# Two output projections as three products of rounded halves, with the waits around them cut finer

## The chip, the cores and the metric

One core of a Trainium2 chip. The time is that of the device for one call of the kernel, in microseconds (us), median of three runs; less is better.

## What is computed

The input x is 8 images of 512 channels and 32 x 32 pixels. Two layers follow each other, both of the form x + attention(group norm(x)):

```python
# layer 0: dense attention over the 1024 pixels, 8 heads of 64
qkv = xs @ Wqkv + bqkv
scores = einsum('bhqd,bhkd->bhqk', q, k) / sqrt(64)
out = einsum('bhqk,bhkd->bhqd', softmax(scores), v)
out = out @ Wout + bout                        # first output projection
# layer 1: deformable attention in 4 x 4 windows of 8 x 8 pixels
xn = layer norm over channels; q = grouped 1x1 of xn (8 groups of 64)
off = tanh(pw(gelu(depthwise 6x6 stride 4 of q))) * 4   # 4 sample points per window and group
kv = grid_sample(xn, off); k, v = grouped 1x1 of kv
bias = MLP(128, 128, 1) of sign(pos) * log1p(|pos|)
out = einsum('bhij,bhdj->bhdi', softmax(q k + bias), v)
out = einsum('bchw,oc->bohw', out, w_out) + b_out       # second output projection
```

All arrays are float32.

## The kernel before

P = 128 partitions; the 512 channels are CT = 4 tiles. The kernel is written by hand engine by engine: each engine's block (`block.sync` for the DMA queue SP, `block.gpsimd` POOL, `block.tensor` PE, `block.scalar` ACT, `block.vector` DVE) is a Python function that issues that engine's instructions in the order in which it runs them, and semaphores tie them together. So an order is changed by moving a call, and a wait by `wait_ge`.

The main loop on every engine runs over the 8 images i. Image i's first attention runs together with rests of image i - 1's second one:

- **First attention**, 32 steps n (4 pairs of heads, 8 blocks of 128 queries). On PE: `scores` (L622, products of halves into a ring of two double banks, `slot(name)`), two `turn`s (L638, the transposed exponentials), every second step a `value_product` (L653), and in the first two of every eight-step group pieces of the next pair's q and k (`piece`, L597). DVE takes the row maxima (L1318), ACT the exponentials (L1041); both copy what PE turned. The piece's weights come from a ring in SBUF, `wqk_ring`, that SP loads from DRAM (`load_wq`, L444). Sums of exponentials go through DRAM to be spread over partitions (`recips_around`, L454 and L459), and DVE multiplies the outputs with them into `attended` (L1342).
- **First projection**: `project` (L588) with the weights `WO0` (SP, L513, loaded into `exps_turned` when the last value product is done), then DVE's `residual` (L1348), the statistics for the group norm and the store of the result. The next image's `values` (L683) are put between on PE.
- **Second attention** of image i - 1: `mlp` (L799, L811 to L813, L821), into whose start the transposes of image i's normed pixels (`pixels`, L767) are woven, `channel` (L778) with an affine step of ACT (L1201, tiles 0 and 2) and DVE (L1385, tiles 1 and 3), `turn_bias`, `queries` (L786), `first_pair` (L597: q and k of the next image's first two heads), `attend` (L866), `apply_values` (L882), and the **second projection**, `output` (L588 again, weights `WO1`, SP L485) with DVE's `result` (L1560) and the store. Between the tiles of that projection DVE runs the convolution of image i (`convolve`, L1393 and L1394, four times), ahead of the next image's first row maxima; PE has the next image's first scores between tile 2 and tile 3.

A **product of halves** is how most float32 products are done here: an operand is split into a part rounded to float32r (a copy by ACT, `high`) and the remainder (a subtraction by DVE, `low`), and high x high, high x low, low x high are summed in PSUM, one pass of PE each. `project` alone takes float32 operands as they are:

```python
mm = pe.matmul(dst[:, 512 * n:512 * n + 512], weights[:, k, n0:n0 + P],
               moving[:, k, 512 * n:512 * n + 512], start=(k == 0), stop=(k == CT - 1))
```

## Time and profile before

| | |
|---|---|
| median of 3 runs | 3527.37 us (3524.6 to 3533.67) |
| the profiled execution's own time | 3524.64 us |
| its span | 3522.8 us |
| granted TensorE clock, mean | 0.981 |
| PE busy | 3264.3 us, 93% |
| DVE busy | 2216.4 us, 63% |
| ACT busy | 1595.2 us, 45% |
| HBM read and written | 145.62 MB and 43.32 MB |

Busy time is the time in which an engine runs an instruction. A matmul's duration reaches from its start to a modelled end, and matmuls in a row overlap, so the time that a block of them takes is read from the start of the first to the start of what follows. The chain that ended last is followed back from the last instruction, at each step to what released it. "Idle before" is how long an engine stood before an instruction, with what ended that wait behind it.

### The profile page before, as it was taken

How to read it: one execution, taken by the hardware profiler on the slowest of the kernel's cores; microseconds unless marked ns; L12 is line 12 of the kernel's file. 1: busy time of each engine (PE TensorE's matmuls, PEld its weight loads, DVE VectorE, ACT ScalarE, POOL GpSimd, SP SyncE). 2: the span in 40 equal slices, each digit the busy share in tenths (PEclk: the TensorE clock that was granted, in tenths of full speed). 3: DMA queues.
4: the chain of work that ended last, by engine and by line, in shares of the span. 5: the costliest groups of instructions: out<-in, count | busy, mean ns of one | idle time of the engine just before them, and what ended most of it. 6: DMA issues, size and time to landing. Idle time of an engine off the chain costs nothing.

```text
span 3522.8 us, 50334 instructions
## 1 busy us (share of the span) xinstructions
PE 3264.3 (93%) x20128; PEld 2160.1 (61%) x20128; DVE 2216.4 (63%) x2981; ACT 1595.2 (45%) x2322; POOL 220.9 (6%) x165
## 2 busy tenths in 40 slices
PE   6999798999989999899999999999999899987978
PEld 5766576556765567655776557765676555764544
DVE  5664567466666666676665856658567576655754
ACT  3541555264543555353552635426355263543533
POOL 0000020000100020000200002000020000200200
PEclk9999899999999999999999999999999999998979
DMA  4112012301123011311012111121112301103020
GB/s 172 30 52 71 16 33 70 103 25 35 33 70 101 31 37 33 99 64 43 26 57 92 46 48 33 56 93 45 38 33 77 103 19 40 34 10 101 24 56 36
DMA packets 142633, 192.21 MB, mean 55 GB/s; under 512 B 80897, under 2 KB 100868, under 8 KB 140836
## 3 DMA queue, kind: packets, MB, share of 16 engines
q1 hardware_dynamic: 142404, 188.99, 17.2%
q8 instruction: 164, 2.69, 0.5%
q14 instruction: 65, 0.53, 0.1%
HBM read 145.62 MB, written 43.32 MB: 54 GB/s over the span
## 4 chain that ended last, share of the span: by engine, by line
PE 80%; DVE 7%; ACT 4%; DMA 4%; issue 3%; SPq 1%; POOL 0%; DVEq 0%; ACTq 0%
PE banks L588 13%; PE banks L638 13%; PE banks L653 12%; PE banks L622 11%; PE banks L597 8%; PE banks L811 4%; PE banks L683 3%; PE banks L821 3%; PE banks L812 3%; PE banks L813 3%; ACT exps L1041 2%; DMA recips_dram<-recips 2%; DVE qk_halves L1487 2%; PE banks L882 2%; PE banks L786 2%
## 5 line engine op out<-in xcount | busy, mean ns | idle before, releaser
L1318 DVE TENSOR_REDUCE neg_max<-banks 128x1 f32<-128x1024 f32 x512 | 601.7, 1216 | 77.7 <-PE banks L622 75.9
L1041 ACT ACTIVATE exps<-banks,neg_max 128x1024 f32<-128x1024 f32 x512 | 564.9, 1111 | 176.7 <-DVE neg_max L1318 175.8
L1051 ACT ACTIVATE exps_turned<-banks 128x1024 f32<-128x1024 f32 x256 | 262.3, 1024 | 780.1 <-PE banks L638 780.1
L638 PE MATMUL banks<-ident,exps 128*128 128x128 f32 x4096 | 554.7, 279 | 56.6 <-ACT exps_turned L1051 43.3
L1327 DVE COPY exps_turned<-banks 128x1024 f32<-128x1024 f32 x256 | 313.3, 1224 | 455.8 <-PE banks L638 455.1
L638 PEld LDWEIGHTS banks<-ident,exps 128*128 128x128 f32 x4096 | 449.6, 141 | 212.6 <-issue 162.1
L653 PE MATMUL banks<-exps_turned,values 128*64 128x256 f32 x4096 | 473.3, 384 | 13.4 <-issue 8.2
L622 PE MATMUL banks<-qk_halves 64*128 64x512 f32 x3072 | 431.4, 412 | 58.3 <-ACT exps L1041 52.7
L653 PEld LDWEIGHTS banks<-exps_turned,values 128*64 128x64 f32 x4096 | 287.8, 137 | 162.7 <-issue 36.1
L622 PEld LDWEIGHTS banks<-qk_halves 64*128 64x128 f32 x3072 | 283.5, 187 | 145.5 <-issue 107.8
L597 PE MATMUL banks<-x_hi,wqk_ring 128*128 128x512 f32 x1024 | 350.2, 406 | 2.8 <-DMA wqk_ring<-wqk_split 2.8
L1487 DVE SCALAR_TENSOR_TENSOR qk_halves<-banks,qk_halves 128x1024 fp32r<-128x1024 f32 x256 | 301.8, 1218 | 78.0 <-ACT qk_halves L1088 77.8
L1088 ACT ACTIVATE qk_halves<-banks 128x1024 fp32r<-128x1024 f32 x256 | 249.4, 1024 | 150.8 <-PE banks L799 150.6
L811 PE MATMUL banks<-qk_halves,mlp_w_hi 128*128 128x512 f32 x512 | 232.9, 455 | 21.4 <-ACT exps L1104 13.6
L588 PE MATMUL banks<-attended,exps_turned 128*128 128x512 f32 x512 | 223.3, 597 | 11.9 <-DMA exps_turned<-in_wo 11.8
L588 PE MATMUL banks<-exps_turned,attended 128*128 128x512 f32 x512 | 222.6, 593 | 0.0
L1184 ACT ACTIVATE normed<-exps,group_shift,group_rstd 128x256 f32<-128x256 f32 x64 | 32.4, 589 | 418.8 <-DVE group_shift L1670 418.8
L597 PEld LDWEIGHTS banks<-x_hi,wqk_ring 128*128 128x128 f32 x1024 | 193.3, 189 | 45.1 <-issue 3.9
L1503 DVE TENSOR_SCALAR exps<-banks,mlp_b 128x512 f32<-128x512 f32 x256 | 190.2, 746 | 33.5 <-PE banks L813 26.8
L812 PE MATMUL banks<-qk_halves,mlp_w_hi 128*128 128x512 f32 x512 | 205.4, 401 | 0.0
L813 PE MATMUL banks<-qk_halves,mlp_w_lo 128*128 128x512 f32 x512 | 204.5, 399 | 0.0
L811 PEld LDWEIGHTS banks<-qk_halves,mlp_w_hi 128*128 128x128 f32 x512 | 98.0, 191 | 169.7 <-ACT exps L1104 117.8
(170 smaller groups left out, 3586.2 us busy)
## 6 DMA issues: line engine op xcount, KB each, us to landing
wqk_ring<-wqk_split SPq DMA_DIRECT2D x64, 512.0 KB, 4.0
recips_b<-recips_dram SPq DMA_DIRECT2D x256, 64.0 KB, 3.5
exps_turned<-in_x SPq DMA_DIRECT2D x32, 512.0 KB, 7.6
x_dram<-exps SPq DMA_DIRECT2D x32, 512.0 KB, 2.6
exps_turned<-x_dram SPq DMA_DIRECT2D x32, 512.0 KB, 5.7
out<-exps_turned SPq DMA_DIRECT2D x32, 512.0 KB, 2.6
x_image<-in_x SPq DMA_DIRECT2D x7, 2048.0 KB, 9.7
wv_halves<-wv_split SPq DMA_DIRECT2D x6, 2048.0 KB, 8.1
```

Of the source, the lines that this page charges most:

```text
L588: mm = pe.matmul(dst[:, 512 * n:512 * n + 512], weights[:, k, n0:n0 + P], moving[:, k, 512 * n:512 * n + 512], start=(k == 0), stop=(k == ...
L597: mm = pe.matmul(dst, WQ[:, w, a, k], half[:, k, c:c + 512], start=(k == 0 and a == 0 and half is XH), stop=(k == CT - 1 and a == 1))
L622: mm = pe.matmul(slot(("s", 2 * n + h, i))[:, 512 * c:512 * c + 512], QK[rows, p % 2, a, P * j:P * j + P], QK[rows, p % 2, b, 512 * c:512 ...
L638: mm = pe.transpose(TB[:, kt // 4, kt % 4 * P:kt % 4 * P + P], PB[:, 2 * h + n % 2, kt * P:(kt + 1) * P], IDENT[:])
L653: mm = pe.matmul(OB[D * h:D * h + D, 0:256], V[:, kt, hc:hc + D], PT[:, u % 2, h, kt], start=(kt == 0), stop=(kt == KT - 1))
L811: pe.matmul(h2_bank(c), W2H[:], h1_hi_half(u)[:, cols], start=True, stop=False)
L812: pe.matmul(h2_bank(c), W2H[:], h1_lo_half(u)[:, cols], start=False, stop=False)
L813: pe.matmul(h2_bank(c), W2L[:], h1_hi_half(u)[:, cols], start=False, stop=True)\
L1041: freed(act.activation(PB[:, 2 * h + n % 2], slot(("s", m, i)), ACT.Exp, bias=NM[:, m:m + 1], accum_out=SS[:, m:m + 1]), ("s", m, i))
L1318: dve.tensor_reduce(NM[:, m:m + 1], slot(("s", m, i)), AX.X, ALU.max, negate=True).then_inc(mx, 1)
L1327: dve.tensor_copy(PT[:, n // 2 % 2, 1, :, P * j:P * j + P], TB.rearrange("p s (k q) -> p (s k) q", k=4)).then_inc(t_free[1], 1)
L1487: freed(dve.scalar_tensor_tensor(out=h1_lo_half(u), in0=slot(("h1", u, j)), scalar=0.0, in1=h1_hi_half(u).bitcast(F32), op0=ALU.max, op1=A ...
```

## The change

1. **Products of halves.** `project` takes weights and moving operand in halves: three products for each of before's, with k now outside of the loop over the two halves of the columns. The weights of both projections are split in image 0's first attention (`wo_high` on ACT, `wo_low` on DVE, at steps 4 and 10), stored to DRAM and loaded from there in each image, 2 MB each instead of 1. What goes in is split per image: `attended_high` (ACT) and `attended_low` (DVE) behind the last step of the attention, `apply_values` on both engines for the second projection, which did two of the four tiles each and now do all four each.
2. **Waits and places.** (a) The first projection waits per channel tile for its halves, and wo0 is loaded when the last but one value product is done. (b) The first pair of image 0 reads its weights where they were split, in SBUF, and not from the ring. (c) `piece(0, i)` goes behind the first turn of step 0, on ACT and DVE too. (d) The first MLP units wait each for its own slot, and the first two blocks of pixel rows are put between them. (e) The affine steps of tiles 0 and 2 go to DVE, 1 and 3 to ACT. (f) The last outputs of an attention stand ahead of the second value bias on DVE. The convolution's scratch moves to the exponentials' buffer.

```diff
+        WO0 = at("wo0_halves", [P, 2, CT, C], AT_PT, F32R)
+        WO1 = at("wo1_halves", [P, 2, CT, C], AT_OT, F32R)
+        WOR = at("wo_raw", [P, CT, C], AT_OT + 8192)
+        WOS = at("wo_split", [P, 2, CT, C], AT_A, F32R)
...
-            load_wq(0, 0)
-            load_wq(1, 0)
             load_wq(2, 0)
             load_wq(3, 0)
+            wait_full(sp, ("k", 0, 0))
+            sp.dma_start(WOR[:], wo0.rearrange("(t p) n -> p t n", p=P)).then_inc(wo_raw, 16)
...
-                sp.dma_start(WO1, woT.rearrange("(t p) n -> p t n", p=P)).then_inc(wo1_in, 16)
+                sp.wait_ge(wo_out, 32)
+                sp.dma_start(WO1[:].bitcast(F32), wo_dram[1]).then_inc(wo1_in, 16)
...
+                    if u in (2, 6) and not i:
+                        sp.wait_ge(wo_lo, 1 if u == 2 else 2)
+                        sp.dma_start(wo_dram[0 if u == 2 else 1], WOS[:].bitcast(F32)).then_inc(wo_out, 16)
...
+                sp.wait_ge(av_full, i * OUTS + OUTS - 1)
+                sp.wait_ge(wo_out, 16)
+                sp.dma_start(WO0[:].bitcast(F32), wo_dram[0]).then_inc(wo0_in, 16)
                 sp.wait_ge(av_full, i * OUTS + OUTS)
-                sp.dma_start(WO0, wo0.rearrange("(t p) n -> p t n", p=P)).then_inc(wo0_in, 16)
...
-                for n in range(2):
-                    for k in range(CT):
+                for k in range(CT):
+                    for n in range(2):
                         if needs:
                             needs(n, k, name[2])
-                        mm = pe.matmul(dst[:, 512 * n:512 * n + 512], weights[:, k, n0:n0 + P],
-                                       moving[:, k, 512 * n:512 * n + 512], start=(k == 0), stop=(k == CT - 1))
+                        for a, half in ((0, hi), (1, hi), (0, lo)):
+                            mm = pe.matmul(dst[:, 512 * n:512 * n + 512], weights[:, a, k, n0:n0 + P],
+                                           half[:, k, 512 * n:512 * n + 512], start=(k == 0 and a == 0 and half is hi),
+                                           stop=(k == CT - 1 and half is lo))
...
             def attended(n, k, i):
-                if n == 0 and k == 0:
-                    pe.wait_ge(ot_done, i * OUTS + 12)
-                elif k == CT - 1:
-                    pe.wait_ge(ot_done, i * OUTS + 14 + 2 * n)
+                if n == 0:
+                    pe.wait_ge(ot_split, CT * i + k + 1)
...
-                piece(0, i)
                 for n in range(STEPS):
                     if n + 1 < STEPS:
                         scores(n + 1, i)
                     turn(n, 0, i)
+                    if n == 0:
+                        piece(0, i)
...
+            def attended_high(t, i):
+                act.wait_ge(ot_done, i * OUTS + 4 * (t + 1))
+                if t == 0 and i + 1 < B:
+                    act.wait_ge(xl_done, (i + 2) * CT)
+                act.activation(OTH[:, t], OT[:, t], ACT.Copy).then_inc(ot_hi, 1)
...
-                for t in (0, 2):
+                for t in (1, 3):
                     wait_full(act, ("tc", t, i))
...
+            def attended_low(t, i):
+                dve.wait_ge(ot_hi, CT * i + t + 1)
+                dve.tensor_tensor(OTL[:, t], OT[:, t], OTH[:, t].bitcast(F32), ALU.subtract).then_inc(ot_split, 1)
...
+                for t in range(CT - 1):
+                    attended_low(t, i)
                 if i + 1 < B:
                     add_value_bias(0, i + 1)
+                outputs(OUTS - 1, i)
+                attended_low(CT - 1, i)
+                if i + 1 < B:
                     add_value_bias(1, i + 1)
-                outputs(OUTS - 1, i)
```

How the order of instructions moves, at three places. SP at the end of image 1's attention (`recips_dram` and `recips_b` are the reciprocals' way through DRAM, `exps_turned<-in_wo` the load of the first projection's weights), before:

```order
L459 DMA recips_b<-recips_dram 64x256
L454 DMA recips_dram<-recips 128x4x1 [waits rc_done]
L459 DMA recips_b<-recips_dram 64x256 [waits ot_done,rc_out1]
L459 DMA recips_b<-recips_dram 64x256
L513 DMA exps_turned<-in_wo 128x4x512 [waits av_full]
L515 DMA exps_turned<-in_x 128x1024 x4
L521 DMA x_dram<-exps 128x1024 [waits ring_free0]
```

and now:

```order
L473 DMA recips_b<-recips_dram 64x256
L468 DMA recips_dram<-recips 128x4x1 [waits rc_done]
L473 DMA recips_b<-recips_dram 64x256 [waits ot_done,rc_out1]
L473 DMA recips_b<-recips_dram 64x256
L534 DMA wo_halves<-wo_split_dram 128x4096 [waits wo_out,av_full]
L537 DMA exps_turned<-in_x 128x1024 [waits av_full]
L537 DMA exps_turned<-in_x 128x1024 x3
L543 DMA x_dram<-exps 128x1024 [waits ring_free0]
```

The load keeps its place behind the reciprocals, but the wait for the last value product (`av_full`) now stands also behind it, ahead of the residual's tiles (`exps_turned<-in_x`).

PE from the last tile of the second projection of image 0 into the attention of image 2 (`exps_turned,attended` are that projection's operands, `qk_halves` the scores, `ident,exps` the turns, `x_hi,wqk_ring` the piece, of which three of its nine rows stand here), before:

```order
L588 MATMUL banks<-exps_turned,attended 128x512 x7
L597 MATMUL banks<-x_hi,wqk_ring 128x512 [waits o1c_done,piece_free,wq_in0]
L597 MATMUL banks<-x_lo,wqk_ring 128x512
...
L597 MATMUL banks<-x_hi,wqk_ring 128x512
L622 MATMUL banks<-qk_halves 128x512 [waits ring_free1,ring_free0]
L622 MATMUL banks<-qk_halves 128x512 x11
L638 MATMUL banks<-ident,exps 128x128 [waits o1d_done,turned_free1,ring_free0]
L638 MATMUL banks<-ident,exps 128x128 x7
L638 MATMUL banks<-ident,exps 128x128 [waits turned_free0,ring_free1]
L638 MATMUL banks<-ident,exps 128x128 x7
L622 MATMUL banks<-qk_halves 128x512 [waits ring_free1,ring_free0]
```

and now (`applied_lo,wo_halves` is the projection's last product):

```order
L611 MATMUL banks<-applied_lo,wo_halves 128x512
L650 MATMUL banks<-qk_halves 128x512 [waits ring_free1,ring_free0]
L650 MATMUL banks<-qk_halves 128x512 x11
L666 MATMUL banks<-ident,exps 128x128 [waits o1d_done,turned_free1,ring_free0]
L666 MATMUL banks<-ident,exps 128x128 x7
L621 MATMUL banks<-x_hi,wqk_ring 128x512 [waits o1c_done,piece_free,wq_in0]
L621 MATMUL banks<-x_lo,wqk_ring 128x512
...
L621 MATMUL banks<-x_hi,wqk_ring 128x512
L666 MATMUL banks<-ident,exps 128x128 [waits turned_free0,ring_free1]
L666 MATMUL banks<-ident,exps 128x128 x7
L650 MATMUL banks<-qk_halves 128x512 [waits ring_free1,ring_free0]
```

The piece has moved from ahead of the scores of step 1 to between the two turns of step 0.

PE at the start of the MLP (`attended,mlp_w_rows` are its first layer, `ident,normed` the pixel rows), before:

```order
L799 MATMUL banks<-attended,mlp_w_rows 128x512 [waits ring_free1,ring_free0,rows_in_first]
L799 MATMUL banks<-attended,mlp_w_rows 128x512 x3
L767 MATMUL banks<-ident,normed 128x128 [waits gn_var,gnorm_act,gnorm_dve]
L767 MATMUL banks<-ident,normed 128x128 x7
L767 MATMUL banks<-ident,normed 128x128 [waits gn_var,gnorm_act,gnorm_dve]
L767 MATMUL banks<-ident,normed 128x128 x7
L767 MATMUL banks<-ident,normed 128x128 [waits pixel_rows_tb_done,gnorm_act,gnorm_dve]
L767 MATMUL banks<-ident,normed 128x128 x7
L767 MATMUL banks<-ident,normed 128x128 [waits pixel_rows_om_done,gnorm_act,gnorm_dve]
L767 MATMUL banks<-ident,normed 128x128 x7
L811 MATMUL banks<-qk_halves,mlp_w_hi 128x512 [waits ring_free0,pixel_rows_tb_done]
```

and now:

```order
L821 MATMUL banks<-attended,mlp_w_rows 128x512 [waits ring_free0,rows_in_first]
L821 MATMUL banks<-attended,mlp_w_rows 128x512
L794 MATMUL banks<-ident,normed 128x128 [waits gn_var,gnorm_act,gnorm_dve]
L794 MATMUL banks<-ident,normed 128x128 x7
L821 MATMUL banks<-attended,mlp_w_rows 128x512 [waits ring_free1]
L821 MATMUL banks<-attended,mlp_w_rows 128x512
L794 MATMUL banks<-ident,normed 128x128 [waits gn_var,gnorm_act,gnorm_dve]
L794 MATMUL banks<-ident,normed 128x128 x7
L794 MATMUL banks<-ident,normed 128x128 [waits pixel_rows_tb_done,gnorm_act,gnorm_dve]
L794 MATMUL banks<-ident,normed 128x128 x7
L794 MATMUL banks<-ident,normed 128x128 [waits pixel_rows_om_done,gnorm_act,gnorm_dve]
L794 MATMUL banks<-ident,normed 128x128 x7
```

Each first unit waits for its own slot alone, and a block of pixel rows stands between the two.

## Rows read from the trace of the kernel before

**Rows 1.** The page, busy time and instructions of the engines.

```profile
PE 3264.3 (93%) x20128; PEld 2160.1 (61%) x20128; DVE 2216.4 (63%) x2981; ACT 1595.2 (45%) x2322; POOL 220.9 (6%) x165
```

**Rows 2.** The page, chain that ended last, by engine.

```profile
PE 80%; DVE 7%; ACT 4%; DMA 4%; issue 3%; SPq 1%; POOL 0%; DVEq 0%; ACTq 0%
```

**Rows 3.** Groups of PE: form xcount | busy us, mean ns | idle before.

```profile
L588 PE MATMUL banks<-attended,exps_turned 128*128 128x512 f32 x512 | 223.3, 597 | 11.9 <-DMA exps_turned<-in_wo 11.8
L588 PE MATMUL banks<-exps_turned,attended 128*128 128x512 f32 x512 | 222.6, 593 | 0.0
...
L683 PE MATMUL banks<-wv_halves,x_hi 128*128 128x512 f32 x512 | 164.1, 402 | 10.6 <-DVE x_lo L1289 10.6
```

**Rows 4.** The chain in order of time (start us, us, what), image 2.

```profile
1063.71 27.73 PE banks L588 x64
1091.44 5.47 PE banks L683 x24
...
1218.45 20.60 PE banks L588 x48
1240.66 7.06 PE banks L588 x16
```

**Rows 5.** Timeline of PE at the start (start us, us, what, [idle before]).

```profile
45.44 0.39 PE L683 MATMUL banks<-wv_halves,x_lo 128*128 128x512 f32 x1
48.64 0.50 PE L597 MATMUL banks<-x_hi,wqk_ring 128*128 128x512 f32 x1 [2.81 <-DMA wqk_ring<-wqk_split]
```

**Rows 6.** Timeline of SP's queue, ends of the attentions of images 2 and 7.

```profile
1054.54 3.24 SPq L459 DMA_DIRECT2D recips_b<-recips_dram  x2
1058.14 0.38 SPq L513 DMA_DIRECT2D exps_turned<-in_wo  x1
...
3175.65 0.59 SPq L513 DMA_DIRECT2D exps_turned<-in_wo  x1
```

**Rows 7.** Timeline of PE, first projection of image 7.

```profile
3183.23 29.16 PE L588 MATMUL banks<-attended,exps_turned 128*128 128x512 f32 x64 [8.52 <-DMA exps_turned<-in_wo]
```

**Rows 8.** DMA issues: count, KB each, median us from issue to landing.

```profile
wv_halves<-wv_split SPq DMA_DIRECT2D x6, 2048.0 KB, 8.1
...
exps_turned<-in_wo SPq DMA_DIRECT2D x8, 1024.0 KB, 5.6
```

**Rows 9.** Timeline of DVE, image 2, end of the attention and second projection.

```profile
1039.60 2.35 DVE L1289 TENSOR_TENSOR x_lo<-x_image,x_hi 128x1024 fp32r<-128x1024 f32 x2
...
1057.23 1.22 DVE L1295 TENSOR_TENSOR values<-banks,b_v 128x1024 f32<-128x1024 f32 x1 [3.88 <-PE banks L653]
...
1219.63 1.82 DVE L1393 TENSOR_TENSOR attended<-normed,conv_w 128x1600 f32<-128x1600 f32 x1
1221.48 1.82 DVE L1394 TENSOR_REDUCE conv_sums<-attended 128x64 f32<-128x1600 f32 x1
1225.41 1.28 DVE L1560 SCALAR_TENSOR_TENSOR exps_turned<-banks,b_out,exps_turned 128x1024 f32<-128x1024 f32 x1 [2.11 <-PE banks L588]
...
1241.98 2.35 DVE L1318 TENSOR_REDUCE neg_max<-banks 128x1 f32<-128x1024 f32 x2
```

**Rows 10.** Timeline of PE, first steps of the attentions of images 1 and 3.

```profile
394.66 2.93 PE L622 MATMUL banks<-qk_halves 64*128 64x512 f32 x12 [13.89 <-ACT exps L1041]
...
1254.29 1.06 PE L638 MATMUL banks<-ident,exps 128*128 128x128 f32 x8 [1.20 <-ACT exps_turned L1051]
1256.48 1.65 PE L622 MATMUL banks<-qk_halves 64*128 64x512 f32 x12 [1.13 <-ACT exps L1041]
```

**Rows 11.** Timeline of PE, start of the MLP and channels, image 2.

```profile
1104.03 0.40 PE L799 MATMUL banks<-attended,mlp_w_rows 21*128 21x512 bf16 x4 [1.41 <-DVE values L1295]
...
1187.49 1.94 PE L778 MATMUL banks<-ident,pixels 128*128 128x128 f32 x16 [0.96 <-ACT normed L1201]
```

**Rows 12.** Timeline of ACT, image 2.

```profile
1035.74 1.06 ACT L1140 ACTIVATE x_hi<-x_image 128x1024 fp32r<-128x1024 f32 x1
...
1186.15 1.20 ACT L1201 ACTIVATE normed<-banks,ln_b_T,ln_w_T 128x1024 f32<-128x1024 f32 x1
```

163 lines of the change are left out of this document (107 added, 56 removed).

## The prediction

> **What bounds the kernel now.** I read the page first. TensorE (PE) is busy for 93% of the span [rows 1], and the chain that ended last lies on PE for 80% [rows 2]. So a microsecond that PE loses or gains in program order is, nearly everywhere, a microsecond of the result; the other engines count only where PE waits for them. Then the groups by line: both output projections are line 588, 512 instructions in each [rows 3]. The chain in order of time shows what one projection costs: 64 instructions in 27.73 us in the first attention [rows 4]. For the price of the new kind of product I looked for a block of the same shape that the kernel has already: behind that projection stand 24 products of rounded halves (values, line 683) in 5.47 us [rows 4]. The rest comes from the timelines around the places where the order changes.
>
> The profiled execution took 3524.64 us, its span is 3522.8, and the median of three runs is 3527.37. The sum is made in differences against this execution and then taken off the median.
>
> **1. The products.** One projection is 4 x 2 x 4 = 32 full float32 products, which the trace shows as 64 instructions: 27.73 us [rows 4], 867 ns each. Now it is 96 products of halves. At 5.47/24 = 0.228 us each [rows 4] that is 21.9 us, 5.8 less. The second projection is the same work, 20.60 us for 48 instructions and 7.07 for 16 [rows 4]. There are 8 images and two projections in each, PE is on the path in all of them: 16 x 5.8 = **92 us less**. The mean of 402 ns that the group of such products shows [rows 3] is the time from a product's start to its end, which overlaps the next one, and isn't what one costs in a row of them. In the same stage one pass of a float32 instruction takes 27.73/128 = 0.217 us, which is the lower bound for a product: 16 x (27.73 - 20.8) = 111 us. The upper bound is 402 ns (below, as the slower case). I take 0.228, since operands, shape and the weight load per product are those of the rows it comes from.
> The Trainium skill (TensorE: Matmul & The Clock Gate, "Wait — 56ns, not 53.3ns?") gives warm matmuls of 512 columns start to start in N/2.4 GHz plus about 2.5 ns, 215.7 ns. By it the first term would be 112 us; the trace's 228 ns does not agree, and I go by the trace.
>
> **2. Splitting what goes in.** Per projection ScalarE (ACT) copies four tiles (1.06 us each [rows 12]) and VectorE (DVE) subtracts four times (2.35/2 = 1.18 us [rows 9]). After the attention, tiles 0 to 2 are ready early; their three remainders take 3.5 us, and DVE idles 3.88 us there before it adds the value bias [rows 9]: hidden, just. The last tile goes outputs, copy, remainder, some 2.7 us behind the landing of the last reciprocals, while PE needs it only at the 19th product, 4.1 us after the projection's start. In the second projection the last copy and remainder end 2.3 us after the last product with v_blocks, again before the 19th: cost 0 on PE. But DVE starts its convolution 1.1 us later than now, which term 5 counts. The weights' split runs in the first attention (two copies and two remainders of twice that size, by the same rows an estimated 2.1 and 2.4 us each), where PE's work covers pauses of both engines: I take 0. If that cover were gone, it would cost 9 us once.
>
> **3. The weights' load.** The halves are 2 MB instead of 1. A 1 MB load of wo0 lands in 5.6 us, the 2 MB load of wv_halves in 8.1 [rows 8]. SP issues it no longer after the last value product but after the one before; that gives less than it seems, since ahead of it on SP's queue stand the last reciprocals, whose two issues end at 1054.54 + 3.24 = 1057.8, against 1058.14 for the load now [rows 6]. So in image 2 it lands at about 1065.8 where the projection started at 1063.71 [rows 4]: 2.1 us lost. In the last image it is issued at 3175.65 [rows 6], and PE waited 8.52 us and began at 3183.23 [rows 7]; with 2.4 us more for the second MB it loses 2.4. The same working gives 0 to 2.4 us in the other six, where the values of the next image cover more: together **11 us more**. If the load took as little as now, the term would be 0; if it took 5 us more than I say, it would be 50. The second load (wo1) has the queries, pairs and attend in front of its use and stays hidden.
>
> **4. The start.** The first pair now reads its weights in SBUF. PE had waited 2.81 us for the ring's load [rows 5]: **2.8 less**, with 0 as the other bound if the last value bias holds it.
>
> **5. The turn from one image to the next** (images 1 to 6). Let T be the start of the second projection, 1218.45. Now DVE does four convolutions of 1.82 + 1.82, and three results of 1.28, between 1219.63 and 1241.98 [rows 9]; it waits for PE's output tiles in between. With faster tiles it is DVE that sets the pace: it starts at T + 2.3, needs about 18.5 us, and finds the row maxima from T + 20.8 on instead of T + 23.5. PE is done with the fourth tile at T + 23.6; the exponentials free the banks at T + 24.3, so the second scores wait 0.7 us. Then piece 0, which stood ahead of them, fills the pauses of 1.20 and 1.13 us that PE had behind them [rows 10]. Scores of step 2 come at T + 30.9 instead of 1256.48 = T + 38.0. That is 7.1 less, of which 5.8 are in term 1: 1.3 x 6 = **8 less**. Bounds: 0, and 2.3 x 6 = 14. Before images 0 and 1 PE had idle time there anyway (13.89 us, DVE convolving [rows 10]) which piece 0 shortened; it no longer does: **1 more** for both.
>
> **6. The finer waits in the second attention.** The MLP's first unit waited 1.41 us for a value bias that only the second needs [rows 11]; now unit 0 and the first pixel rows go ahead: 1.3 x 6 = **8 less** (bounds 0 and 8.5). Behind the MLP, PE waited 0.96 us for ACT's affine tile [rows 11], which stood on ACT behind the copy of the bias rows and started at 1186.15 [rows 12]. It is DVE's now, with no such copy in front of it: 0.96 x 7 = **7 less** (bounds 0 and 7). What is late next is the bias softmax, and queries and the first pair stand in front of that.
>
> **Sum**: -92 + 0 + 11 - 3 - 8 + 1 - 8 - 7 = -106 against the profiled execution; off the median, 3527.4 - 106 gives 3421 us.
>
> **The rivals.**
> A. The finer waits gain nothing, because the wait only moves to the next engine (DVE carries four remainders more per stage and is in order), and the load is later by 3 us per image than I say. For it: DVE already sets the pace at T. Against: the releasers in rows 10 and 11 are the very ones taken away. -92 - 3 + 35 + 1 = -59: 3468. With only one of the two, 3444.
> B. The products come faster than in the rows, at the 0.217 us of a float32 pass. For: it is the same array and the same 512 columns. Against: 24 products in 5.47 us, wherever the chain shows them. -111 in place of -92: 3402. (The Trainium skill's rule above says the same, to 1 us; that rule has the chance of this case.)
> C. Slower. The new loop takes the two halves of the columns inside the k loop, so PE changes its PSUM bank after every three products and goes on accumulating in a bank it left; nothing in the trace does that with such products. If it kept a product from overlapping the next, each would cost up to its 402 ns [rows 3]: 38.6 us a projection, 10.9 more than now, 16 x 10.9 = 174 more, less 14 for the other terms: 3687. It decides from 27.73/96 = 0.289 us a product on. Against: scores and value products change banks between instructions and still run at PE's pace.
> D. The change doesn't do what it says. The products are in the program; but the earlier load may be none, since the queue holds it back. That is in term 3 already and has no chance of its own.
>
> **The numbers.** With terms 2 to 6 at their worst (9 + 50 + 0 + 1 + 0) term 1 still leaves 32 us, so the sign hangs on the price of a product alone. Forecast 0.66, A 0.19 (a third of that beyond 3446), B 0.12, C 0.02, and 0.01 for a product at about 0.289 us, which ends within 0.3%. What differs by less than 0.3% (10.6 us) can't be told from no change here. The range from 3402 to 3446 takes in B, half-way A, and terms 3 to 6 between their nearer bounds. Faster 0.97, same 0.01, slower 0.02.
>
> **What would show it.** Line 611 in blocks of 96 products in 21.9 us, right also where it alternates banks; 24.8 us or more would say term 1 is wrong by half. PE waiting for the load of the halves 3 to 4 us in most images and some 11 in the last. Scores of step 2 at T + 31, with DVE's row maxima as the releaser of a wait under 1 us. No wait of 1.4 us ahead of the MLP's first unit, none of 0.96 at the channels, and no wait for the ring at the start. The forecast is wrong if the sum of PE's waits grows by more than 30 us, or if the granted clock of a projection falls to its lower level in more images than the last.

## The result and the profile after

The changed kernel takes **3446.09 us** (median of 4 runs, 3441.39 to 3453.51), the kernel before 3526.95 in the same comparison (4 runs, 3524.6 to 3533.67): ratio 0.977, 95% interval 0.9751 to 0.9789. The forecast was 3421, so the sign and the size of the main term were right and 25 us of the gain are missing; the time lies on the upper end of the range (3446), not inside it with room to spare. The profiled execution of the changed kernel took 3447.59 us with a span of 3445.5, which is 77.3 less than the span before; the sum had said 106 less.

The page after, busy time of the engines and the chain by engine, beside [rows 1, 2]:

```profile
PE 3187.0 (92%) x20640; PEld 2263.2 (66%) x20640; DVE 2278.8 (66%) x3031; ACT 1645.1 (48%) x2372; POOL 220.9 (6%) x165
...
PE 75%; DVE 10%; DMA 7%; ACT 4%; issue 3%; SPq 1%; POOL 0%; DVEq 0%; ACTq 0%
```

PE's share of the chain fell from 80% to 75%, and DMA's rose from 4% to 7%. So part of what PE gave up was taken over by transfers: by the load of the halves, and by the store of the reciprocals, which stands ahead of that load in SP's queue (`recips_dram<-recips`, 2% of the page's chain before and 4% after). The chain in order of time shows both, at the same place as [rows 4]:

```profile
1047.68 10.68 DMA wo_halves<-wo_split_dram
1058.41 23.66 PE banks L611 x96
1082.08 5.44 PE banks L711 x24
...
3261.48 21.82 PE banks L611 x96
```

A block of 96 products in the second projection takes 21.82 us, as forecast (21.9). The same block in the first projection takes 23.66, and a load of 10.68 us stands ahead of it. PE's waits (us in total, times, longest us) name that load third:

```profile
PE banks L650 <- ACT exps L1075: 56.3, 42, 17.0
PE banks L666 <- ACT exps_turned L1085: 33.6, 33, 1.2
PE banks L611 <- DMA wo_halves<-wo_split_dram: 30.1, 7, 8.7
```

It was 11.8 us in 4 waits for wo0 before, the longest 8.5. SP's queue, where [rows 6] has the load at 1058.14 and 3175.65, issues it right behind the last reciprocals, images 2 and 7:

```profile
1046.49 1.09 SPq L473 DMA_DIRECT2D recips_b<-recips_dram  x2
1047.68 0.53 SPq L534 DMA_DIRECT2D wo_halves<-wo_split_dram  x1
...
3112.05 1.08 SPq L473 DMA_DIRECT2D recips_b<-recips_dram  x2
3113.23 0.53 SPq L534 DMA_DIRECT2D wo_halves<-wo_split_dram  x1
```

And the stretches of the eight first projections show what the granted clock does there (columns: stretch, its length, busy time and instructions of PE, PEld, DVE, ACT and POOL, granted clock, DMA share, GB/s):

```profile
309.00:334.00 25.00, 24.13 (x94) 19.71 (x95) 7.71 (x9) 0.00 (x0) 0.00 (x0) 0.86 0.36 145
643.00:668.00 25.00, 24.18 (x100) 19.91 (x101) 8.35 (x10) 0.00 (x0) 0.00 (x0) 0.93 0.29 119
1058.00:1083.00 25.00, 24.59 (x101) 20.20 (x102) 8.60 (x10) 0.00 (x0) 0.00 (x0) 0.93 0.28 113
1473.00:1496.00 23.00, 23.00 (x103) 19.06 (x102) 9.80 (x11) 0.00 (x0) 0.00 (x0) 1.00 0.31 126
1888.00:1913.00 25.00, 24.17 (x100) 19.84 (x100) 8.20 (x10) 0.00 (x0) 0.00 (x0) 0.93 0.35 143
2300.00:2324.00 24.00, 23.22 (x102) 19.22 (x103) 8.80 (x10) 0.00 (x0) 0.00 (x0) 1.00 0.35 142
2713.00:2738.00 25.00, 24.89 (x98) 20.36 (x99) 7.82 (x10) 0.00 (x0) 0.00 (x0) 0.88 0.27 111
3122.00:3146.00 24.00, 23.44 (x96) 18.97 (x96) 8.18 (x10) 0.00 (x0) 0.00 (x0) 0.94 0.33 135
```

Below 1.00 the clock spends part of the stretch at its lower level, 1.2 GHz. Only the image at 1473, where PE did not wait for the load, and the one at 2300, with the shortest wait (2.34 us), stay at 2.4 GHz throughout; the other six waited 3.25 to 8.67 us. In the runs below, waits of 2.3 to 2.7 us went both ways: the block behind one took 21.9 us in some images and 23.3 to 24.7 in others.

Stage by stage, the two traces differ as follows (starts of the same blocks on PE, changed kernel minus kernel before, summed over the images they concern):

| stretch | forecast | measured |
|---|---|---|
| the 16 projections, if all ran at the upper clock level | -92 | -94 |
| lower clock level in the first projections | 0 (not in the sum) | +12 |
| PE's start of the first projection, against the last value product (8) | +11 | +18.4 |
| image 0's attention (reciprocals and the next image's pixels late) | 0 | +8.8 |
| start of the kernel up to image 0's scores of step 2 | -3 + 0.5 | -1.5 |
| turns into images 1 to 7, beside the projection | -8 + 0.5 | -7.3 |
| start of the MLP, beside the projection | -8 | -9.1 |
| MLP to the channels | 0 | +4.6 |
| channels to the second projection (7) | -7 | -7.4 |
| the other attentions and the rest | 0 | about -2 |

For the first line I added up the pieces of the chain: the kernel before has 444.0 us in 16 projections; now the eight second ones take 8 x 21.82 = 174.6 and the eight first ones 187.7, against 175.2 if each took 21.9.

Image 0's attention shows two waits that the sum did not have. The first, in DVE's timeline, before:

```profile
120.27 0.39 DVE L1342 TENSOR_TENSOR attended<-banks,recips_b 128x256 f32<-128x256 f32 x1
133.76 0.40 DVE L1342 TENSOR_TENSOR attended<-banks,recips_b 128x256 f32<-128x256 f32 x1
```

After:

```profile
119.68 0.42 DVE L1399 TENSOR_TENSOR attended<-banks,recips_b 128x256 f32<-128x256 f32 x1
138.34 0.42 DVE L1399 TENSOR_TENSOR attended<-banks,recips_b 128x256 f32<-128x256 f32 x1 [5.12 <-DMA recips_b<-recips_dram]
```

SP's queue in that stretch of the changed kernel:

```profile
116.42 0.58 SPq L518 DMA_DIRECT2D wo_split_dram<-wo_split  x1
117.04 0.43 SPq L520 DMA_DIRECT2D wo_raw<-in_woT  x1
119.77 0.36 SPq L468 DMA_DIRECT2D recips_dram<-recips  x1
133.29 1.09 SPq L473 DMA_DIRECT2D recips_b<-recips_dram  x2
```

The reciprocals are 2 KB. Issued at 119.77 behind a store of 2 MB and a load of 1 MB, they land only 13.5 us later, and SP stands until then. The page's median for that store is 8.4 us. At PE this costs 4.0 of the 8.8 us, at steps 12 and 13; 0.9 are lost at step 7.

The second wait costs the other 3.9, at steps 27 and 28. DVE wants the next image's pixels for its statistics, and their load (2 MB) lands 13.9 us after its issue, where it took 9.8 in the kernel before:

```profile
228.67 0.59 SPq L528 DMA_DIRECT2D x_image<-in_x  x1
```

```profile
242.57 2.47 DVE L1321 BATCH_NORM_STATS2 bn_stats<-x_image 128x6 f32<-128x512 f32 x4 [3.93 <-DMA x_image<-in_x]
```

Nothing large stands directly ahead of this load: the second store of split weights had landed at 186.9.

### The profile page after: what moved, and what is told of

It is laid out like the page before. It is cut to its first block, busy times and chain, and to the rows that moved or that the text cites. A ratio compares the mean times of both kernels' runs of the same rounds, so it can differ in the third digit from the quotient of the medians.

```text
span 3445.5 us, 51484 instructions
## 1 busy us (share of the span) xinstructions
PE 3187.0 (92%) x20640; PEld 2263.2 (66%) x20640; DVE 2278.8 (66%) x3031; ACT 1645.1 (48%) x2372; POOL 220.9 (6%) x165
## 4 chain that ended last, share of the span: by engine, by line
PE 75%; DVE 10%; DMA 7%; ACT 4%; issue 3%; SPq 1%; POOL 0%; DVEq 0%; ACTq 0%
PE banks L666 12%; PE banks L681 12%; PE banks L650 11%; PE banks L611 9%; PE banks L621 8%; PE banks L840 4%; DMA recips_dram<-recips 4%; PE banks L850 3%; PE banks L841 3%; PE banks L842 3%; PE banks L711 2%; DMA wo_halves<-wo_split_dram 2%; DVE qk_halves L1546 2%; PE banks L916 2%; ACT exps L1075 2%
## 5 line engine op out<-in xcount | busy, mean ns | idle before, releaser
L621 PE MATMUL banks<-x_hi,wqk_ring 128*128 128x512 f32 x992 | 336.9, 403 | 0.0
L840 PE MATMUL banks<-qk_halves,mlp_w_hi 128*128 128x512 f32 x512 | 234.0, 457 | 20.7 <-ACT exps L1138 13.5
L621 PEld LDWEIGHTS banks<-x_hi,wqk_ring 128*128 128x128 f32 x992 | 186.4, 188 | 38.3 <-issue 1.7
L611 PE MATMUL banks<-attended_hi,wo_halves 128*128 128x512 f32 x512 | 167.3, 409 | 30.1 <-DMA wo_halves<-wo_split_dram 30.1
L621 PE MATMUL banks<-x_lo,wqk_ring 128*128 128x512 f32 x496 | 193.7, 391 | 0.0
L1138 ACT ACTIVATE exps<-banks,mlp_b 128x512 f32<-128x512 f32 x256 | 168.5, 693 | 32.1 <-PE banks L842 31.7
## 6 DMA issues: line engine op xcount, KB each, us to landing
exps_turned<-in_x SPq DMA_DIRECT2D x32, 512.0 KB, 10.3
x_image<-in_x SPq DMA_DIRECT2D x7, 2048.0 KB, 10.3
```

Of the source, the lines that this page charges most:

```text
L611: mm = pe.matmul(dst[:, 512 * n:512 * n + 512], weights[:, a, k, n0:n0 + P], half[:, k, 512 * n:512 * n + 512], start=(k == 0 and a == 0 a ...
L621: mm = pe.matmul(dst, weights[:, a, k], half[:, k, c:c + 512], start=(k == 0 and a == 0 and half is XH), stop=(k == CT - 1 and a == 1))
L840: pe.matmul(h2_bank(c), W2H[:], h1_hi_half(u)[:, cols], start=True, stop=False)
```

## The experiments

The times are medians. There were four comparisons, each with the kernel before beside it: the load first and the three single waits (before: 3524.1 us); the half load, the pieces, the spread store and the three waits together (3526.0); the filled wait and the free place (3523.6); the last two kernels once more (3525.6). The changed kernel ran in none of these four; beside it the kernel before took 3526.95, so a difference to the changed kernel can carry up to 3.4 us of the difference between comparisons.

### Is it the place of the load in the queue?

```diff
                 for u in range(OUTS):
+                    if u == OUTS - 1:
+                        sp.wait_ge(av_full, i * OUTS + OUTS - 1)
+                        sp.wait_ge(wo_out, 16)
+                        sp.dma_start(WO0[:].bitcast(F32), wo_dram[0]).then_inc(wo0_in, 16)
                     recips_around(u, i)
...
-                sp.wait_ge(av_full, i * OUTS + OUTS - 1)
-                sp.wait_ge(wo_out, 16)
-                sp.dma_start(WO0[:].bitcast(F32), wo_dram[0]).then_inc(wo0_in, 16)
                 sp.wait_ge(av_full, i * OUTS + OUTS)
```

> The changed kernel with one edit: SP issues the load of the first projection's halves ahead of the last reciprocals (it waits for value product 14 alone), not behind them. In the changed kernel PE waits 2.3 to 4.3 us for this load in six images and 8.7 in the last, and the granted clock falls to its lower level inside the projection that follows, which then takes 22.1 to 24.9 us instead of 21.8. Theory Q (the load's place in SP's queue costs both): the load lands before PE asks, PE's wait for it falls from 30 us in all to under 4, the projections of images 0 to 6 take 21.8 us each, and the time falls by 20 to 28 us, to about 3421. Theory M (the 2 MB compete with the reciprocals' own transfers, so that the wait only moves to them): the last reciprocals land some 5 us later, PE waits for the split of the last tile instead, and the time falls by under 8 us.

Measured: 3417.44 us (3416.43 to 3419.26), ratio 0.9698 (0.9683 to 0.9712), 28.7 less than the changed kernel. SP's queue at the end of the attention of image 2:

```profile
1028.89 1.24 SPq L473 DMA_DIRECT2D recips_b<-recips_dram  x2
1030.24 0.53 SPq L516 DMA_DIRECT2D wo_halves<-wo_split_dram  x1
1030.83 0.42 SPq L468 DMA_DIRECT2D recips_dram<-recips  x1
1044.88 2.84 SPq L473 DMA_DIRECT2D recips_b<-recips_dram  x2
```

The load goes out some 15 us before the issue of the last reciprocals' broadcast that it stood behind, and PE waits for it nowhere. The waits ahead of the first projection are 33.0 us shorter in sum. The last image pays part of that back, as theory M has it, because now the reciprocals stand behind the 2 MB. DVE's timeline there:

```profile
3080.84 3.48 DVE L1623 TENSOR_TENSOR attended_lo<-attended,attended_hi 128x1024 fp32r<-128x1024 f32 x3
3094.20 0.42 DVE L1400 TENSOR_TENSOR attended<-banks,recips_b 128x256 f32<-128x256 f32 x1 [9.88 <-DMA recips_b<-recips_dram]
3095.75 1.22 DVE L1623 TENSOR_TENSOR attended_lo<-attended,attended_hi 128x1024 fp32r<-128x1024 f32 x1 [1.12 <-ACT attended_hi L1187]
```

PE then waits 6.72 us in the middle of the projection for the fourth tile's remainder. In the other images the next image's value products cover most of this; two waits of 1.2 us are left.

### Or its size?

```diff
-                sp.dma_start(WO0[:].bitcast(F32), wo_dram[0]).then_inc(wo0_in, 16)
+                sp.dma_start(WO0[:, 0].bitcast(F32), wo_dram[0][:, 0]).then_inc(wo0_in, 16)
...
-                            mm = pe.matmul(dst[:, 512 * n:512 * n + 512], weights[:, a, k, n0:n0 + P],
+                            mm = pe.matmul(dst[:, 512 * n:512 * n + 512], weights[:, 0 if name and name[0] == "o0" else a, k, n0:n0 + P],
```

> The changed kernel, its load of the first projection's weights where it was, but of the rounded halves alone (1 MB instead of 2); the products that took the remainders take the rounded halves again, so that their number is the same and the remainders' part of the first projection is left out. Theory B (the bytes set the landing): the landing falls from 8 to about 5 us, the waits for wo_halves from 30 us in sum to 5 to 12, time 3422 to 3430. Theory F (place in the queue and a fixed delay set it): landing still 7 to 8 us, waits still over 22 us in sum, time 3440 to 3447.

Measured: 3420.10 us (3414.74 to 3422.1), ratio 0.9685 (0.9646 to 0.9724). PE's waits and the landing:

```profile
PE banks L611 <- DMA wo_halves<-wo_split_dram: 12.3, 4, 8.0
```

```profile
wo_halves<-wo_split_dram SPq DMA_DIRECT2D x8, 2048.0 KB, 7.6
wo_halves<-wo_split_dram SPq DMA_DIRECT2D x8, 1024.0 KB, 6.2
```

This kernel leaves out the remainders' part of the first projection's weights and is a probe of the load alone. Theory B: the waits return to what the kernel before had (11.8). The landing shortened by less than I said: 6.2 us, not 5, where the first projection's eight loads in the changed kernel take 7.9 to 11.2, with a median of 8.7 (the page's 8.0 mixes in those of the second). A little was enough. The time fell by 26, more than the 18 of the waits; the next experiment shows why.

### What does the clock cost behind the wait?

```diff
+                wait_free(pe, ("o0", 0, i))
+                for _ in range(15):
+                    pe.matmul(slot(("o0", 0, i))[:, 0:512], XH[:, 0, 0:P], XH[:, 0, 0:512], start=True, stop=True)
                 pe.wait_ge(wo0_in, 16 * (i + 1))
```

> The changed kernel with 15 more products of 512 columns (values nobody reads, into the bank that the projection then starts afresh) between the next image's value products and the wait for the first projection's halves: 15 x 0.228 = 3.4 us of work in the place of a wait of 3 to 4 us; the load is where it was. Theory G (the wait costs twice: its own length, and the lower granted clock behind it, 187.9 us for the eight blocks of 96 products where eight at 21.96 would be 175.7): the waits for wo_halves fall to under 12 us in sum, the products start when they did, and six or seven of the blocks come down to 22.0: 8 to 12 us less from the clock, up to 2 us more in the image whose load was in time, 3436 to 3441. Rival (the clock falls for another reason, such as the kind of product): blocks stay at 23.5 to 24.9, time 3446 to 3452.

Measured: 3440.61 us (3437.37 to 3447.11), ratio 0.9764 (0.975 to 0.9778), 5.5 less than the changed kernel though PE does 120 products more. The two intervals overlap (0.9751 to 0.9789 for the changed kernel), so it is the trace that decides here. By it the stretch from the start of the first projection to the MLP is 10.4 us shorter in sum, and PE's start of the projection is unchanged (+0.6 in sum). The first four of its stretches and the last:

```profile
315.00:338.00 23.00, 22.87 (x101) 18.63 (x100) 7.94 (x10) 0.00 (x0) 0.00 (x0) 1.00 0.38 155
646.00:669.00 23.00, 23.00 (x104) 19.03 (x103) 7.97 (x10) 0.00 (x0) 0.00 (x0) 1.00 0.36 140
1058.00:1081.00 23.00, 22.92 (x102) 18.89 (x102) 8.43 (x10) 0.00 (x0) 0.00 (x0) 1.00 0.36 149
1472.00:1495.00 23.00, 23.00 (x103) 19.04 (x102) 8.72 (x10) 0.00 (x0) 0.00 (x0) 1.00 0.23 92
...
3117.00:3141.00 24.00, 23.40 (x96) 18.95 (x96) 8.16 (x10) 0.00 (x0) 0.00 (x0) 0.94 0.35 142
```

Seven of the eight are at 1.00 now, and their blocks take 21.8 to 22.1 us. The eighth kept a wait of 5.04 us, longer than the filling, and its clock. So the wait costs twice: by its length, and by 1.5 to 3 us of the lower clock behind it. The whole trace is only 4.9 us shorter: 2.3 of the 10.4 are taken back in the attentions, where image 0 is 5.0 longer (DVE waits 7.18 us for the next image's pixels instead of 3.93) and others are shorter, and the rest at the start, at the first turn and inside the MLP. The Trainium skill (TensorE: Matmul & The Clock Gate, "HAM oscillation — how this bites in real kernels") describes a kernel in which a wait for a transfer ahead of each tile makes each tile start at the lower level; the trace agrees, at 0.86 to 0.94 in six of the eight first projections, and at 1.00 in the seven whose wait is filled.

### The load in pieces around the reciprocals

```diff
+            def load_wo0(t):
+                sp.dma_start(WO0[:, :, t].bitcast(F32), wo_dram[0][:, :, t]).then_inc(wo0_in[t], 16)
...
+                    if u == OUTS - 1:
+                        sp.wait_ge(av_full, i * OUTS + OUTS - 1)
+                        sp.wait_ge(wo_out, 16)
+                        load_wo0(0)
+                        load_wo0(1)
                     recips_around(u, i)
...
+                load_wo0(2)
+                load_wo0(3)
...
                 if n == 0:
+                    pe.wait_ge(wo0_in[k], 16 * (i + 1))
                     pe.wait_ge(ot_split, CT * i + k + 1)
```

> The changed kernel with the load of the first projection's halves in four pieces of 512 KB, one for each 128 input channels: two ahead of the last reciprocals, two behind them, each waited for by itself. Theory H (a big load ahead holds up the small reciprocals behind it): with the whole load ahead the last image's reciprocals came 9.9 us late and PE waited 6.7 us for the split of the fourth channel block; with half the bytes ahead that wait falls to under 3 us and no load is waited for: 3408 to 3413. Rival L: the third and fourth piece come too late for the first block of 24 products (5.5 us): 1 to 3 us of waits for wo_halves in each image, and the granted clock falls again behind them: 3422 to 3440.

Measured: 3419.52 us (3414.94 to 3442.62), ratio 0.9694 (0.965 to 0.9738), no better than the whole load ahead, and nearer to rival L. PE waits 10.8 us in 7 waits for the pieces, 5.93 of it in the last image. SP's queue there says why:

```profile
3082.83 1.22 SPq L498 DMA_DIRECT2D wo_halves<-wo_split_dram  x2
3084.09 0.60 SPq L468 DMA_DIRECT2D recips_dram<-recips  x1
3094.38 1.11 SPq L473 DMA_DIRECT2D recips_b<-recips_dram  x2
3095.53 1.25 SPq L498 DMA_DIRECT2D wo_halves<-wo_split_dram  x2
```

My edit put the second pair of pieces behind the place where SP stands and waits for the reciprocals to land in DRAM, so they go out 12.7 us after the first. What the rows do show is the price of what stands ahead. From the issue of the 2 KB store to the issue of what waits for it take 3094.38 - 3084.09 = 10.3 us behind 1 MB, 11.8 behind 2 MB (the last image of the run with the whole load ahead, 3077.17 to 3089.00), 7.9 with neither in front (3082.61 to 3090.51 in the run with the half load). The order holds over all eight images, with some spread: 10.3 to 12.0 us for the last store of an image in this run, 12.7 to 14.4 in images 0 to 6 of the run with the whole load ahead, issued there 0.6 to 0.9 us before the store and in the last image 3.2 before it, and 7.8 to 10.5 in the changed kernel.

### Image 0: the store of the split weights in pieces

The weights' split was as in the change; only its transfers are cut, on top of the early load (the second split runs at step 14 instead of 10, since its raw weights come later):

```diff
-                    if u in (2, 6) and not i:
-                        sp.wait_ge(wo_lo, 1 if u == 2 else 2)
-                        sp.dma_start(wo_dram[0 if u == 2 else 1], WOS[:].bitcast(F32)).then_inc(wo_out, 16)
-                    if u == 2 and not i:
-                        sp.dma_start(WOR[:], woT.rearrange("(t p) n -> p t n", p=P)).then_inc(wo_raw, 16)
+                    if 2 <= u < 10 and not i:
+                        k, t = (u - 2) // 4, (u - 2) % 4
+                        if t == 0:
+                            sp.wait_ge(wo_lo, k + 1)
+                        sp.dma_start(wo_dram[k][:, :, t], WOS[:, :, t].bitcast(F32)).then_inc(wo_out, 16)
+                        if k == 0:
+                            sp.dma_start(WOR[:, t], woT.rearrange("(t p) n -> p t n", p=P)[:, t]).then_inc(wo_raw, 16)
```

> The changed kernel with the first projection's halves loaded ahead of the last reciprocals (as in the run that took 3417.4 us), and in image 0 the split weights stored, and the second raw weights loaded, in four pieces of 512 KB each over reciprocals 2 to 9 instead of 2 MB and 1 MB at once behind reciprocals 2 and 6. Theory S: the first attention of the changed kernel lost 8.8 us (12.5 in the run with the early load) because the 2 KB of reciprocals stand behind 2 MB in the same queues; pieces let them through: image 0's stretch from the scores of step 2 to the last value product 6 to 12 us shorter than in the run with the early load, no wait of the vector engine for reciprocals over 3 us at 137 us, time 3406 to 3411. Theory N: that loss is the split's own work on the scalar and vector engines, or chance in the transfers: 3415 to 3419 and the waits stay.

Measured: 3408.91 us (3402.22 to 3425.86), ratio 0.9666 (0.962 to 0.9711). The stretch from image 0's scores of step 2 to its last value product takes 215.0 us; it is 213.9 in the kernel before, and 222.7 to 228.7 in each of the nine traces that have the split with its large transfers (the changed kernel and eight of the experiments). The same kernel once more:

> The kernel with the early load and the split's transfers in pieces, once more, so that it stands in one comparison with the next run. If its median of 3408.9 us with runs from 3402 to 3426 was spread and not its time, it comes to 3402 to 3409; image 0's attention again takes 215 to 216 us, not 222 or more.

Measured: 3412.44 us (3404.29 to 3414.98), ratio 0.9676 (0.9661 to 0.9692), with 215.7 us for that stretch. The median is 3 us above the range that I expected. DVE's rows at the place shown above, in the first of the two, without a wait:

```profile
120.75 0.39 DVE L1402 TENSOR_TENSOR attended<-banks,recips_b 128x256 f32<-128x256 f32 x1
134.23 0.39 DVE L1402 TENSOR_TENSOR attended<-banks,recips_b 128x256 f32<-128x256 f32 x1
```

That is what theory S forecast, and theory N falls: the split's own work on ACT and DVE costs at most the 1 to 2 us that are left. But the mechanism of S, small reciprocals behind a large store, covers only a part of the gain. It is 3.6 to 5.8 us at steps 12 and 13 in the nine traces with large transfers. A further 3.7 to 8.0 us (8.0 in the run with the early load, most of what was won on it) is lost there at steps 27 and 28, to the wait for the next image's pixels. Their load lands 13.2 to 16.4 us after its issue in those nine traces, and after 8.1 to 11.0 in the kernel before and in the four with pieces. So that wait goes with the large transfers too, though none stands ahead of the load in its queue; by which way is open.

### The finer waits, one group at a time

First piece back ahead of step 1:

```diff
+                piece(0, i)
                 for n in range(STEPS):
                     if n + 1 < STEPS:
                         scores(n + 1, i)
                     turn(n, 0, i)
-                    if n == 0:
-                        piece(0, i)
```

(and `high_piece(0, i)` and `low_piece(0, i)` on ACT and DVE likewise)

> The changed kernel with piece 0 back in its old place on PE, ACT and DVE, ahead of the scores of step 1. My theory: it refills a pause of 0.7 us and opens the two of 1.2 and 1.1 us again, so each of images 2 to 7 loses about 1.5 us and images 0 and 1 win 0.5 each: 8 us slower, 3454, with the scores of step 2 some 31 + 1.5 us behind T. The rival (DVE sets the pace at the turn and the place of the piece is idle): no difference beyond 2 us.

Measured: 3455.31 us (3452.22 to 3465.34), ratio 0.9802 (0.9787 to 0.9817), 9.2 more. Scores of step 2 are 1.65 us later in each of images 2 to 7, 9.9 in sum, and 1.9 earlier in image 0.

The MLP's first units and the pixels back in their old order:

```diff
-                for u in range(2):
-                    wait_free(pe, ("h1", u, j))
-                    mlp1_unit(u)
-                    if i is not None:
-                        pixels(u, i)
+                mlp1(0)
                 if i is not None:
+                    pixels(0, i)
+                    pixels(1, i)
                     pixels(2, i)
```

> The changed kernel with the start of the MLP as before: both first units wait for both slots, and all four blocks of pixel rows come behind. My theory at the prediction: 1.3 us in each of images 1 to 6 are lost, 8 us slower, 3454. The rival, from the changed kernel's trace (the stretch from the MLP's first unit to the channels grew by 0.6 to 1.1 us in four images): a part of it is given back inside the MLP, where ACT and DVE set the pace, and only 3 to 5 us are lost.

Measured: 3456.88 us (3453.96 to 3460.8), ratio 0.981 (0.9794 to 0.9825), 10.8 more. The wait that the change had removed is back, in PE's timeline of image 2:

```profile
1098.81 0.40 PE L821 MATMUL banks<-attended,mlp_w_rows 21*128 21x512 bf16 x4 [1.41 <-DVE values L1350]
```

From the projection's last product to the MLP's first it takes 12.94 us instead of 11.47 in each of images 1 to 6, 8.8 in sum. The MLP behind it is 1.3 shorter in sum, with 0.1 to 1.9 either way in each, so little or nothing is given back there.

The channels' affine steps back to ACT for tiles 0 and 2, DVE for 1 and 3:

```diff
-                for t in (1, 3):
+                for t in (0, 2):
                     wait_full(act, ("tc", t, i))
...
-                for t in (0, 2):
+                for t in (1, 3):
                     affine(t, i)
```

> The changed kernel with the affine steps back on the engines of before (ACT tiles 0 and 2, DVE 1 and 3). My theory: PE's wait of 0.96 us at the third channel tile comes back in 7 images, 7 us slower, 3453; the trace of the changed kernel shows 0.6 us gained at the queries and another 0.5 up to the second projection, 1.1 in all. The rival (the bias softmax is what PE waits for behind the queries, so the channels' wait is free): under 2 us.

Measured: 3454.36 us (3443.02 to 3461.74), ratio 0.9799 (0.9778 to 0.9819), 8.3 more with a wide spread, and an interval that meets the changed kernel's; by its own stretch 4.5 (0.60 us at the queries in each of 7).

All three undone together, the edits of the three diffs above in one kernel (ACT's and DVE's parts too):

```diff
+                piece(0, i)
                 for n in range(STEPS):
...
+                mlp1(0)
...
-                for t in (1, 3):
+                for t in (0, 2):
                     wait_full(act, ("tc", t, i))
```

> The changed kernel with the three groups of finer waits that were undone singly now undone together (first piece back ahead of step 1, the row products and the pixels in their old order, the affine steps of the channels in their old order): what is left is the projections of three products, their weights' load, the split and the start. Theory of the sum: the singles cost 9.2, 10.8 and 8.3 us (9.2, 5.8 and 4.5 by their own stretches of the trace), so 3466 to 3474. Rival A (each of these waits hides behind the next one when another is there): under 3455.

Measured: 3467.6 us (3460.3 to 3480.12), ratio 0.9825 (0.9783 to 0.9866), 21.5 more than the changed kernel. The stretches of the three single runs sum to 9.9 - 1.9 + 8.8 + 4.5 = 21.3, their times to 28.3. The waits add, and rival A's idea that each hides behind the next falls; the stretches were the better measure of each, the single medians carried some 2 us each of other things. (The sum of stretches that I wrote down before the run, 9.2 + 5.8 + 4.5, had the MLP's start too small: its 5.8 took in the first projections, which ran at a higher mean clock in that trace.)

### The last image's load in a free place

The last image has no next image, so the buffer of the value weights is free from the time at which the others load it:

```diff
+                    elif u == 12:
+                        sp.wait_ge(kvt_full, 2 * i)
+                        sp.dma_start(WV[:].bitcast(F32), wo_dram[0]).then_inc(wo0_in, 16)
...
-                    project(("o0", t, i), WO0, P * t, OTH, OTL, needs=attended if t == 0 else None)
+                    project(("o0", t, i), WO0 if i + 1 < B else WV, P * t, OTH, OTL, needs=attended if t == 0 else None)
```

> The kernel with the early load and the spread split (3408.9 us), and in the last image, which has no next image's value weights to load, the first projection's halves go into the value weights' place behind reciprocals 12, some 50 us before they are needed. Theory: the last image's wait of 3.7 us for the split of the fourth channel block and of 2.0 for the load go (the reciprocals no longer stand behind 2 MB there), its block of 96 falls from 29.3 us to 24 or less; 6 to 9 us less, 3400 to 3403. Rival: the last image's end of the attention waits for the reciprocals and the split by itself, whatever is in the queue: the block still starts with waits of 3 us or more, 3407 to 3411.

Measured: **3398.67 us** (3396.32 to 3409.09), ratio 0.9648 (0.9633 to 0.9664). The mechanism is only partly the one I named. The wait for the load is gone, but PE still waits for the split of the fourth tile:

```profile
PE banks L617 <- DVE attended_lo L1628: 6.1, 3, 4.1
```

With nothing large in front the reciprocals still take 8.5 us from 3066.95 on SP's queue to 3075.46, and the copy, the multiplication and the remainder follow. The block of 96 takes 28.05 us, where I had said 24 or less. The wait of 4.1 us is that of the rival. The two profiled executions had spans of 3400.6 and 3400.2 us, so I ran this kernel beside the one without the edit:

> The kernel whose last image's load goes into the value weights' place, once more beside the run before it. Theory: its own stretches were 5 us shorter (start of the last projection 2.0, block and MLP start 1.3, up to the channels 1.6), so 4 to 6 us less than the run beside it. Rival: the two are equal within 2 us, as the spans of their first profiled executions were (3400.2 and 3400.6), and the difference of 10 us between their medians was between comparisons.

Measured: 3401.83 us (3397.28 to 3414.16), ratio 0.9645 (0.9632 to 0.9658), against 3412.44 and 0.9676 (0.9661 to 0.9692) beside it. The intervals do not meet: it is the fastest kernel of this study, 44 us below the changed one. But its own stretch, from the last image's last value product to its channels, took 120.2 and 121.3 us in its two traces and 125.1 and 122.9 in those of the kernel without it, 1.6 to 4.9 less, and neither expectation gave the 10.6 us between the medians. The remainder stays unexplained.

## Why the prediction was right, and where it was not

**Term 1, the products (-92): right.** The block of 24 products of the same shape gave 0.228 us a product, and 96 of them take 21.82 us. That they change banks after every three costs nothing: rival C is out. Rival B is out too, at 0.227 a product.

**What bounded the kernel at the turn: right.** DVE sets the pace at the turn as term 5 had it. It finds the row maxima from 1228.12, 21.25 us after the second projection's start at 1206.87 (forecast 20.8), and the scores of step 2 come at T + 31.2 (forecast 30.9). DVE's timeline and PE's, image 2 into 3, beside [rows 9, 10]:

```profile
1209.67 1.82 DVE L1452 TENSOR_TENSOR exps<-normed,conv_w 128x1600 f32<-128x1600 f32 x1
...
1228.12 2.35 DVE L1375 TENSOR_REDUCE neg_max<-banks 128x1 f32<-128x1024 f32 x2
```

```profile
1231.85 1.66 PE L650 MATMUL banks<-qk_halves 64*128 64x512 f32 x12 [0.82 <-ACT exps L1075]
...
1238.10 1.66 PE L650 MATMUL banks<-qk_halves 64*128 64x512 f32 x12
```

**Term 3, the weights' load (+11): undersized, 18.4, and blind to its second half.** The working took 8.1 us for 2 MB from one median and the start of PE as fixed. The load landed in 10.68 us in image 2. Image by image the start is later by 2.3, 4.4, 2.8, -0.2, 4.2, 2.5, 2.3 and 0.2 us: in the last image, where I put 2.4, nothing is lost, and three of the others lose more than the 2.4 that I allowed at most. The prediction's own signs had it: waits of 3 to 4 us in most images and some 11 in the last are about 30 in sum, which is what came, 18 more than before, and term 3 took 11. And I took the queue place for given: the step "that gives less than it seems, since ahead of it on SP's queue stand the last reciprocals" was right, and should have raised the question what a load ahead of them would do. The answer was 28.7 us.

**The clock (+12): not in the sum.** The text named it as a sign of being wrong ("if the granted clock of a projection falls to its lower level in more images than the last"), and that is what happened in five more images; but no term priced it. By that sign the sum's mechanism is wrong here, whatever the time says. The other sign did not appear: PE stood idle for 258.5 us of the span before and for 258.5 after. The 30.1 us of waits ahead of the blocks cost 12 more behind them. The filled wait shows that the cause is the pause, not the products.

**Term 2, the splits (0): right for the engines, wrong for the queue (+8.8).** I had asked which pauses of ACT and DVE cover four instructions and had not asked what stands in SP's queue behind 2 MB. That is 4.0 of the 8.8; 3.9 more are the next image's pixels, landing late in a way that no term had. The bound of 9 us, for a cover that is gone, meets the 8.8 by luck.

**Terms 4 and 6:** the start gave 1.5 instead of 2.3 net. In the two runs with the first piece back, the scores of image 0's step 2 come at 72.4 and 72.7 instead of 74.2 (75.7 before): term 4's 2.8 us came in full, 3.1 to 3.4, and the piece's new place costs image 0 some 1.7, where term 5 had 0.5. In the second attention the MLP's start gave 8.8 and the affine swap 4.5 by their own experiments, for 8 and 7 forecast. The 4.6 that the MLP itself is longer stood in no term; it is between 1.4 and 5.5 in the 13 traces with the change, and its cause is open. The affine swap left a wait of 0.51 us where 0.96 had been; PE's timeline beside [rows 11]:

```profile
1177.62 1.06 PE L805 MATMUL banks<-ident,pixels 128*128 128x128 f32 x8 [0.51 <-ACT normed L1258]
```

So the part of rival A that came true is its second clause, the later load, not the first.

**Luck.** Four losses stood in no term or too small in one: 7 of the start, 12 of the clock, 9 in image 0, 5 in the MLP. Together they are 33 us, which makes 3454 of the forecast's 3421, past the range. Nearly all of what brings it back to 3446 is small change: 2 us more from the products, 1 at the MLP, and 6.0 in image 1's attention, which in the one trace of the kernel before had a wait of 8.8 us for reciprocals that the change did not aim at. And the upper bound of 3446 was set for rival A and for terms 3 to 6 at their nearer bounds, not for these.

**What the runs of one kernel differ by.** The attentions of images 1 to 6 take 221.0 us in many cases and more in others, for the same instructions. The 14 traces have 15 that are more than 3 us longer (one is image 1 of the kernel before, 6.0), and in each PE falls behind where DVE waits for a transfer: 2.6 to 7.0 us for the next image's pixels, or 8.0 to 9.7 for reciprocals. The two longest are 231.0 (image 2, the spread store run again, with one wait of 8.9 for reciprocals) and 237.3 (image 1, the free place run again, with 8.0 for reciprocals and 7.0 for the pixels). Why a transfer lands late in one execution and not in the next is open; no run varied it.

## What to carry to other kernels

When a change makes PE's work shorter, list every transfer that the work used to cover and where it stands in its queue; here the order of two issues was worth a third of what the arithmetic was. Price a wait ahead of a long block of products twice, once for its length and once for the clock behind it; here the second part was 1.6 to 3.0 us behind each wait of 3.25 us or more in the changed kernel. And small transfers on which a chain of waits hangs must not follow large ones that nobody needs soon: cut the large ones, or issue them where nothing small comes next.

## What the hardware showed unexpectedly

A store of 2 KB that took 7.9 us with nothing large in front, from its issue to the issue of what waits for it, took 10.3 us behind 1 MB, 11.8 behind 2 MB issued 3.2 us before, 12.7 to 14.4 behind 2 MB issued 0.6 to 0.9 us before, and 13.5 behind a 2 MB store and a 1 MB load issued within 3.4 us of it. The Trainium skill (DMA: Bandwidth & Descriptors, "Queues, rings and completion order") has each DMA engine take up descriptors in the order of its ring. The figures agree in direction with a small transfer that queues behind a large one, and the growth is less than the large transfer's whole length.

The loads of 2 MB of halves from DRAM landed between 7.5 and 11.2 us after their issue in one execution of the changed kernel (16 loads, median 8.0). A term that rests on a median of landings needs some 3 us on top as its bound.
